# Attention layers: weighted values packed from 32-row slots into dense chunks by transfers on the chip

## What is computed

```
x = x + L0_attn(norm(x))                 # causal, 16 heads of 16, rotary positions
x = x + L0_xattn(norm(x), ctx, ctx)      # cross attention, 120 keys
x = x + L0_ffn(norm(x))                  # PEER: product keys, top 10 of 8 heads
x = x + L1_attn(norm(x))                 # scores + 0.1 near the diagonal ("band")
x = x + L1_xattn(norm(x), ctx)           # BiDAF-like
x = x + L1_ffn(norm(x))                  # mixture of 8 experts, top 2
```

```
scores = einsum('bhqd,bhkd->bhqk', Q, K) / sqrt(d)
attn   = softmax(scores, axis=-1)
heads  = einsum('bhqk,bhkd->bhqd', attn, V)
out    = heads.transpose(0, 2, 1, 3).reshape(B, S, D) @ Wo.T (+ bo)
```

## Time and profile before

| | us |
|---|---|
| median of 3 runs | 4157.63 |
| lowest and highest run | 4150.65, 4161.31 |
| the profiled execution | 4160.81 |
| its span | 4159.0 |
| TensorE busy in the span | 3525.1 (85%) |
| VectorE busy | 3019.0 (73%) |
| GpSimd busy | 1653.8 (40%) |
| ScalarE busy | 1115.0 (27%) |

### The profile page before, as it was taken

How to read it: one execution, slowest core, us unless ns; L and a number is a source line. 1 busy time by engine, 2 the same in 40 slices (tenths; PEclk the granted TensorE clock), 3 DMA queues, 4 the chain that set the end, 5 groups by cost and what they waited for, 6 DMA issues and landing times. The chain is left out here.

```text
span 4159.0 us, 99218 instructions
## 1 busy us (share of the span) xinstructions
PE 3525.1 (85%) x34064; PEld 2955.9 (71%) x34065; DVE 3019.0 (73%) x11795; ACT 1115.0 (27%) x2400; POOL 1653.8 (40%) x1626
## 2 busy tenths in 40 slices
PE   6999958886699888989999989788786887799998
PEld 4777735554688888888888888555554666588887
DVE  6777736666999999999999999499996444533332
ACT  1333324442222222222222222144443211122221
POOL 3222222220666666666666667532230000133332
PEclk8999978898799999999999999899998886799999
DMA  5333333332000000000000000233331003566565
GB/s 149 87 94 89 82 89 90 92 92 99 2 2 2 3 3 3 2 3 2 2 2 3 2 2 2 67 96 94 84 93 34 9 8 133 151 166 174 166 165 131
DMA packets 238915, 267.28 MB, mean 64 GB/s; under 512 B 37697, under 2 KB 182593, under 8 KB 238049
## 3 DMA queue, kind: packets, MB, share of 16 engines
q1 hardware_dynamic: 224737, 243.38, 19.8%
q0 software_dynamic: 13824, 19.18, 2.9%
HBM read 190.06 MB, written 72.42 MB: 63 GB/s over the span
## 5 line engine op out<-in xcount | busy, mean ns | idle before, releaser
L1118 POOL TENSOR_TENSOR peer_hot_v<-peer_hot_e,peer_parts 80x512 bf16<-80x512 bf16 x768 | 1037.2, 1376 | 503.6 <-DVE peer_hot_e L1157 502.6
L963 PE MATMUL peer_ps_u<-peer_up,peer_g 128*128 128x256 f32 x2048 | 544.3, 414 | 0.6 <-DVE x_all L1274 0.6
L944 PEld LDWEIGHTS peer_ps_h<-peer_xnT,peer_down 128*128 128x128 f32 x4096 | 512.5, 197 | 16.3 <-DMA peer_down<-in_peer_down 0.7
L944 PE MATMUL peer_ps_h<-peer_xnT,peer_down 128*128 128x128 f32 x4096 | 511.0, 279 | 0.3 <-DMA peer_down<-in_peer_down 0.3
L954 PE MATMUL peer_ps_w<-peer_hot_v,peer_hot_u 80*128 80x32 bf16 x12288 | 347.4, 177 | 183.7 <-DVE peer_g L1169 89.1
L954 PEld LDWEIGHTS peer_ps_w<-peer_hot_v,peer_hot_u 80*128 80x128 bf16 x12288 | 335.2, 97 | 210.2 <-DVE peer_hot_u L1161 113.9
L963 PEld LDWEIGHTS peer_ps_u<-peer_up,peer_g 128*128 128x128 f32 x2048 | 404.8, 207 | 54.5 <-issue 1.0
L1041 ACT ACTIVATE peer_g<-peer_ps_h 128x512 f32<-128x512 f32 x256 | 152.9, 597 | 899.3 <-PE peer_ps_h L944 899.2
L1161 DVE TENSOR_TENSOR peer_hot_u<-peer_count,peer_uvT 80x2048 bf16<-80x2048 bf16 x256 | 344.5, 1346 | 0.0
L1929 PE MATMUL moe_ps_t<-moe_xgT,moe_w 128*128 128x128 f32 x2304 | 275.4, 278 | 0.0
L1929 PEld LDWEIGHTS moe_ps_t<-moe_xgT,moe_w 128*128 128x128 f32 x2304 | 265.2, 193 | 4.3 <-issue 0.2
(11 more groups left out here) (362 smaller groups left out, 7249.9 us busy)
## 6 DMA issues: line engine op xcount, KB each, us to landing
moe_w<-in_moe_w SPq DMA_DIRECT2D x144, 512.0 KB, 4.7
causal_qs<-causal_qscratch SPq DMA_DIRECT2D x32, 384.0 KB, 3.8
cross_qs<-cross_qscratch SPq DMA_DIRECT2D x32, 384.0 KB, 3.4
band_qs<-band_qscratch SPq DMA_DIRECT2D x32, 384.0 KB, 3.8
moe_w<-in_moe_w SPq DMA_DIRECT2D x8, 1024.0 KB, 9.3
causal_qscratch<-causal_part SPq DMA_DIRECT2D x32, 192.0 KB, 2.0
causal_kscratch<-causal_part SPq DMA_DIRECT2D x32, 192.0 KB, 2.0
causal_ks<-causal_kscratch SPq DMA_DIRECT2D x32, 192.0 KB, 4.2
```

Source lines behind the costliest of these rows:

```text
L944: mm = nc.tensor.matmul(ps_h[:, n % 2, k * P:(k + 1) * P], down[:, c, 4 * n + k, :], xnT[:, par, c, :], start=(c == 0), stop=(c == DC - 1))
L963: mm = nc.tensor.matmul(ps_u[:], g[:, par, v, :], up[:, v, :], start=(v == 0), stop=(v == EV - 1))
L1118: ins = nc.gpsimd.tensor_tensor(hot_v[0:SEL, n % RING, part], hot_e[0:SEL, n % RING], w, ALU.mult)
```

## The change

Only `attention_stage` and the constants change. A new buffer oqp has two chunks of 128 rows (and two copies, by the parity of the batch): row 16h + e of the heads without gaps. SP's `weigh` moves the values there from oq, SBUF to SBUF, once the second quad of a pair is in oq: for j = 2 (step 13) the rows of quads 0 and 2, for j = 3 (step 1 of the next macro) those of quads 1 and 3. Each time these are four transfers, one for a slot g, of 16 rows x 2 x 1 KB = 32 KB. wo is loaded without the zero rows, in two chunks and not four; `spread` has two matrices and not four. `normalise` stands in step 5, and is two matmuls into ps_n and one product; it waits for the moves (`gathered`). `out` has four matmuls. ps_o is no longer used for spreading. ScalarE's copy to oq[:, 0, :] waits for the moves and the sums of the batch before.

```diff
-        w["wo"] = sb("wo", [P, NQUAD, D])
+        w["wo"] = sb("wo", [P, DC, D])
-        spread = sb("spread", [P, NQUAD, P])
+        spread = sb("spread", [P, DC, P])
+        oqp = sb("oqp", [P, 2, DC, S])
-        onT = sb("onT", [P, NQUAD, S])
+        onT = sb("onT", [P, DC, S])
+        NORMALISE = 5
+        MOVES = 16 * HEADS // 2
-                    if s == 3:
-                        e.normalise(b - 1)
+                    if s == NORMALISE:
+                        e.normalise(b - 1, 1 - par)
...
@@ SP @@
+                def weigh(self, b, par, j):
+                    if j < 2:
+                        return
+                    settle(oq_ready, NQUAD * b + j + 1)
+                    for g in range(4):
+                        at = 4 * HD * (j % 2) + HD * g
+                        sp.dma_start(oqp[at:at + HD, par, :, :],
+                                     oq[SLOT * g:SLOT * g + HD, j % 2:NQUAD:2, :]).then_inc(gathered, 16)
...
@@ TensorE @@
                 def weigh(self, b, par, j):
-                    if j == 0:
-                        wait(pe, on_ready, 2 * b)
...
-                def normalise(self, b):
+                def normalise(self, b, par):
                     pe.wait_ge(rr_ready, b + 1)
-                    for half, bank in enumerate((ps_n, ps_o)):
-                        for n in range(2):
-                            mm = nc.tensor.matmul(bank[:, n * S:(n + 1) * S], spread[:, 2 * half + n, :], rr[:],
-                                                  start=True, stop=True)
-                        mm.then_inc(spread_done, 1)
+                    for c in range(DC):
+                        mm = nc.tensor.matmul(ps_n[:, c * S:(c + 1) * S], spread[:, c, :], rr[:], start=True, stop=True)
+                    mm.then_inc(spread_done, 1)
...
                     for t in range(TT):
-                        for j in range(NQUAD):
-                            mm = nc.tensor.matmul(ps_p[:, 0, t * D:(t + 1) * D], onT[:, j, t * P:(t + 1) * P],
-                                                  w["wo"][:, j, :], start=(j == 0), stop=(j == NQUAD - 1))
+                        for c in range(DC):
+                            mm = nc.tensor.matmul(ps_p[:, 0, t * D:(t + 1) * D], onT[:, c, t * P:(t + 1) * P],
+                                                  w["wo"][:, c, :], start=(c == 0), stop=(c == DC - 1))
...
@@ ScalarE, weigh @@
                     if j == 0:
-                        wait(act, on_ready, 2 * b)
+                        wait(act, gathered, MOVES * b)
+                        wait(act, packed, b)
+                        wait(act, y_used, b)
...
@@ VectorE, normalise @@
                     wait(dve, y_done, b)
-                    for half, bank in enumerate((ps_n, ps_o)):
-                        dve.wait_ge(spread_done, 2 * b + half + 1)
-                        nc.vector.tensor_tensor(onT[:, 2 * half:2 * half + 2, :], oq[:, 2 * half:2 * half + 2, :],
-                                                bank[:].rearrange("p (j s) -> p j s", j=2), ALU.mult).then_inc(on_ready, 1)
+                    dve.wait_ge(gathered, MOVES * (b + 1))
+                    dve.wait_ge(spread_done, b + 1)
+                    nc.vector.tensor_tensor(onT[:], oqp[:, par], ps_n[:].rearrange("p (c s) -> p c s", c=DC),
+                                            ALU.mult).then_inc(on_ready, 1)
```

24 lines of the change are left out of this document (11 added, 13 removed).

## The result

| | before | after |
|---|---|---|
| median of the runs, us | 4159.47 (4150.65 to 4170.31, 4 runs) | 4068.16 (4060.99 to 4071.97, 4 runs) |
| ratio after / before | | 0.9769, 95% interval 0.9748 to 0.9791 |
| span of the profiled execution, us | 4159.0 | 4069.5 |

A forecast was written before the change was run, and what follows sets the result against it. TensorE was taken to bound causal, VectorE band, and a chain of short waits cross. 15 x (2.5 + 2.2 + 1.86) = 98.4, plus 12 and 3, less 5, gave 108 off 4160.8: 4053, stated as 4050 us for the median, range 4020 to 4100.

The forecast's parts named there:

- L: Moves' time from the end of the last issue to landing, taken as 2.0 us; cross just even, causal and band covered.
- The new wait for the stack: TensorE at step 0 waiting for the stack transfer: 0.75 us a batch in causal, 1.75 in cross, mostly absorbed.
- Rivals C and D: Moves land late: C, L is 4.0, 4089 us, 10%; D, overheads add up, L is 6.5, 4178 us, 4%.
- 5 taken off for collisions: VectorE at step 5: small collisions, 5 us taken off the summed gain of 113 us.
- 15 x: All three attention stages: the gain a batch multiplied by fifteen, with the last batch counted in the ends.
- the sign against the forecast that was asked for (below 0.95): TensorE's granted clock in causal falling below 0.95 would show the forecast wrong and the clock rival true.
- 2.2: Cross: gain of 2.2 us a batch from 2.65 us less TensorE work, with bounds 0.9 and 3.0.
- this idle time absorbs the other 1.75 us, since the VectorE chain ahead of it does move: Cross: TensorE's 1.67 us idle before the transposes takes up the new stack wait.
- Rival A: Stack transfers become the bound, nothing absorbed: causal 1.9, cross 0.9, band 1.86 us a batch; 4073 us, 14%.
- VectorE is the bound there: Band: VectorE bound, gaining 0.60 us of work and a 1.26 us wait for the projection, 1.86 a batch.
- Rival B: TensorE's clock in causal and band may fall once every batch, costing 33 us: 4083 us, 10%.
- Ends of stages: After the last batch the serial chain shortens 4 us a stage, 12 in all; smaller weight loads give 3 more.

The follow-up runs named there:

- experiment 4: Changed kernel with the eight matmuls of each output projection run twice: 4132.18 us, ratio 0.9927.
- experiment 1, e1_no_moves: Changed kernel without its eight moves a batch and the waits for them, normalising product reading a constant: 4064.54 us, ratio 0.9765.
- experiment 5: Place of normalise: kernel before with it at step 5 instead of 3, 4248.49 us; changed kernel with it back at step 3, 4142.33 us.
- e10_after_step3: Changed kernel with normalise back at step 3 instead of 5, moves kept: 4142.33 us, ratio 0.9952.
- e6_norm_first: Changed kernel with VectorE's normalised rows for batch b+2 ahead of its steps on the maxima at step 0: 4047.55 us, ratio 0.9723.
- e5_stack_half: Changed kernel, stack's first half waiting for its own parts only, three transfers issued between the maxima's two, the fourth behind them: 4076.47 us, ratio 0.9794.
- experiment 6, e11_before_norm: Kernel before with VectorE's normalised rows ahead of its steps on the maxima at step 0: 4128.90 us, ratio 0.9918.
- experiments 2 and 3: Stack transfer issued earlier: changed kernel 4109.40, 4109.62 with earlier projections, kernel before 4177.60; changed kernel with stack split 4076.47, VectorE's rows first 4047.55, both 4040.54 us.
- e7_both: Changed kernel with the edits of e5_stack_half and e6_norm_first together: 4040.54 us, ratio 0.9702.
- e2_gap: Changed kernel with the stack transfer of batch b+2 issued between the two transfers of the maxima at step 9, not after them: 4109.40 us, ratio 0.9873.
- e12_pool: e6_norm_first with the stack's first half (four transfers a batch) issued by GpSimd on its own queue: 4048.77 us, ratio 0.9734.

## Why the prediction was right, and where 18 us went

**Right.** TensorE's time is the gain: experiment 4 puts 1.76 of the 2.65 us back and 1.57 to 1.71 of them return (the spread's 0.89 and VectorE's product weren't put back by themselves). The moves are covered (experiment 1), in band by their place, while in the other two stages step 3 would have cost next to nothing (experiment 5). The two terms behind that were both off, and about cancel: four moves take 2.5 us of issue and not 1.4 to 1.8, and L, from the end of the last issue to landing, is 1.4 and not 2.0. Where VectorE waits for them in e10_after_step3 (cross) the rows are:

```profile
735.78 2.53 SPq L430 DMA_DIRECT2D cross_oqp<-cross_oq  x4
739.68 0.69 DVE L759 TENSOR_TENSOR cross_onT<-cross_oqp,cross_ps_n 128x512 f32<-128x512 f32 x1 [1.98 <-DMA cross_oqp<-cross_oq]
```

(From its own issue a move lands after 2.0 to 2.7 us by the medians.) The new wait for the stack was put at 0.75 and 1.75 us and is 0.7 and 1.9 (6.3 us in nine causal batches); VectorE's wait for the projection in band is gone. Rivals C and D fall with the landing time. On the rule that spoke against these transfers (the Trainium skill, "DMA: Bandwidth & Descriptors", rules for kernel authors: under 64 KB mostly overhead): the trace agrees that size hardly counts there (32 KB land in 2.0 us, the 128 KB of cross_qscratch in 2.1), but 128 of them in a stage cost nothing that the medians tell, since their fixed times overlap each other and other work.

**The total is in part luck.** 4068 lies in the range with terms that are off both ways: causal 7 us and cross 9 too high, band 7 too low; the ends and the weights 8 too high, and 5 taken off for collisions that didn't come. That is 12 of the 18 us; the rest is the 7 us that the untouched stretches took longer in the profiled executions, which can't be told from no effect.

**Causal, forecast 37.5, measured 30.6.** The batch was right, 2.56 for 2.5. The failed step is "15 x": the first two intervals of the stage gained 0.2 and 2.1 us and the last three 1.6, 1.1 and 0.0. Ten gain in full, not fifteen. The clock has part in it: the first interval went from 0.99 to 0.94 and the last from 1.00 to 0.90, the sign against the forecast that was asked for (below 0.95), but outside the steady batches. An interval at 0.94 or 0.95 is the long one in other kernels too (31.05 us, the second of e6_norm_first; 31.18, the second of e1_no_moves), and e5_stack_half, with 1.00 there, has 27.98 us for the changed kernel's first 30.69. In the last macros there is also nothing left to project or to find, so that TensorE has less to do there; how the missing gain is shared between the two was not tried.

**Cross, forecast 33, measured 23.9.** The failed term is 2.2, it is 1.67. Of 2.65 us, 0.60 didn't come off TensorE's busy time and 0.38 went into new idle time. The forecast had 0.45 for idle time, so that part came true, and nothing for the clock, which was a rival for causal and band alone. (In causal 0.21 didn't come off either, at a clock of 1.00, so about 0.4 of the 0.60 is the clock's, by that comparison.) Two readings behind it need putting right. The earlier trace rows showed one batch of 22.90 us at a clock of 0.95, but cross batches alternate between 22.9 and 24.9, with a mean clock of 0.89: the sum was made on the better half. And "this idle time absorbs the other 1.75 us, since the VectorE chain ahead of it does move" is true of this change, by the waits above (10.2 us gone, 10.8 come), but the idle time was not free: taking it away by itself gives cross 1.07 us a batch in the kernel before (experiment 6). In the changed kernel it is gone, and the same edit gives 0.16. The maxima, the stack and the rows end so close to each other there that moving one makes TensorE wait for another (experiments 2 and 3). Rival A's 0.9 (nothing absorbed) is further off on the other side.

**Band, forecast 28, measured 35.4.** The failed step is "VectorE is the bound there", with 1.86. VectorE kept 1.35 us of idle time in each batch after the change (290.35 less 276.81, by ten), and TensorE's matmuls are priced at 1.5 to 1.6 us of 1.76 by experiment 4. The batch gained 2.13. VectorE's busy time fell by 1.11 us a batch with one instruction less of 0.69; what the rest is was not looked into.

**Rival B**, the clock, was given 10% for causal and band and happened in cross and band, at 0.4 to 0.7 us a batch: the upper figures are the whole shortfall in busy time, the lower ones that less causal's 0.21. Causal stayed at 1.00 in its steady batches. It is the largest thing that the forecast left out, 13 to 20 us over the two stages, an estimate from these figures. What brings it in is only half settled: not the missing projection matmuls (experiment 4, clock 0.82 with them), but the place of normalise alone is enough in the kernel before (experiment 5, 0.83), and in e7_both, which has as much idle time in other places, it is back (0.89, 4.7 us a batch at the lower level). The Trainium skill, "TensorE: Matmul & The Clock Gate", section on HAM oscillation, has idle gaps between bursts as the cause. The trace agrees in part: with 5.7 us of idle time in a cross batch of e2_gap the clock is 0.79, but e11_before_norm has 2.5 us for 3.7 and stays at the 0.89 of the kernel before. Which gap of steps 10 to 15 decides was not isolated.

**Ends of stages, forecast 12 and 3 for the weights, measured 6.5 and 0.6.** Causal gave its 4. Cross gave 1.1: its last projection had run at the full clock before and runs at the lower one now, with half as many matmuls in the same time. First before, then after:

```profile
984.43 3.72 PE L559 MATMUL cross_ps_p<-cross_wo,cross_onT 128*128 128x256 f32 x16 [0.78 <-DVE cross_onT L748]
```

```profile
923.29 3.78 PE L568 MATMUL cross_ps_p<-cross_wo,cross_onT 128*128 128x256 f32 x8 [1.88 <-DVE cross_onT L759]
```

The price of the moves, which were said to run beside the reciprocal there, is the 1.82 us of VectorE above. The 5 us for collisions at step 5 weren't there. The stretch from the last reciprocal of cross to the first of band, nearly all of it the untouched PEER stage, took 1754.6 us before and 1759.3 after; over the other kernels it lies between 1753.3 and 1762.6 without any order, so these 5 us can't be told from no effect. (PEER itself, from the first instruction of its norm to that of band's, took 1663.3 and 1668.4.) The same holds behind band's last reciprocal: 968.0 and 969.1 us to the end of the span, 961 to 976 in the others.

## What to carry to other kernels

A wait that the profile shows may absorb another one and still not be free: see what its chain starts from, and price it by moving it. A transfer that is just in time shows no wait at all, so moving another one in front of it is a change with two sides. A gain per batch is multiplied by the batches that are steady, read over a whole number of periods. Moving a step may leave the rest at a lower clock, so busy time of the same matmuls is to be held against the clock before a loss is put down to a wait. The best version found here is e7_both, 0.9702 of the kernel before.

## What the hardware showed that was not expected

- Issuing a transfer of 16 x 2 x 256 floats from SBUF to SBUF costs 0.6 us of SyncE's queue, four of them 2.5 us, where the stack's cost 0.31 to 0.45 each (forecast: 1.4 to 1.8 for four). The row is one of e5_stack_half; the changed kernel's are alike:

```profile
776.53 2.53 SPq L432 DMA_DIRECT2D cross_oqp<-cross_oq  x4
```

- A 12 KB transfer issued behind 384 KB and more was there after 3.8 us, where 2.1 are enough in the changed kernel, and with the large ones on another engine's queue a write of 12 KB still took 4.1 us instead of 1.6 to 2.1. So the stack and the maxima can't be separated by queues here.
- GpSimd issues the same transfers in 0.54 us (cross_qs) and 0.50 (each cross_ks), against 0.31 and 0.45 on SyncE's queue, and cross_qs lands 4.6 us after its issue there and 3.6 here (medians of e12_pool).
- Half the matmuls of a projection (8 records for 16, at the end of cross) took the same 3.8 us: 0.23 us a record before and 0.47 after, the two levels of the clock.
